# Two loops over groups of tiles and of experts written out in a kernel of four attention and four feed-forward layers

## The reference, cut to what matters

```
x = x + tanh(g_xattn[i]) * xattn_i(layernorm(x), ctx)
x = x + tanh(g_ffn[i])   * ffn_i(layernorm(x))          # i = 0..3
```

```
# ffn_2: 16 experts, 4 chosen per token, hidden width 176, and a shared part
probs = softmax(x @ Wg.T);  w, sel = top_k(probs, 4)
routed = sum over chosen e of w_e * (silu(x @ W1[e].T) * (x @ W3[e].T)) @ W2[e].T

# ffn_3: 64 experts, 8 chosen per token, hidden width 96, at most 128 tokens per expert
g, u = split(x @ gate_up[e]);  out += w_e * (silu(g) * u) @ down[e]
```

## Time and profile before

| | |
|---|---|
| median of 3 runs | 3113.04 us (3112.49 to 3119.17) |
| the profiled execution | 3111.15 us |
| its span, first to last instruction | 3109.1 us |
| busy: PE, DVE, ACT, POOL | 2461.1, 1349.5, 1225.0, 1111.9 us |
| instructions executed in it | 43759 |
| mean granted TensorE clock | 0.897 |

### The profile page before, as it was taken

The page is one execution under the profiler, slowest core; times in us unless marked ns, Lnnn a source line. Parts: engine busy times, 40 slices in busy tenths (PEclk is TensorE's granted clock), DMA queues, the critical chain, the costliest instruction groups (busy, mean ns, idle before and its releaser), DMA issues.

```text
span 3109.1 us, 43759 instructions
## 1 busy us (share of the span) xinstructions
PE 2461.1 (79%) x10553; PEld 1494.0 (48%) x10597; DVE 1349.5 (43%) x3445; ACT 1225.0 (39%) x4408; POOL 1111.9 (36%) x1106
## 2 busy tenths in 40 slices
PE   5999999788888999899999978888758654614553
PEld 4666668443443444466666644444434323303442
DVE  2444333666666333344444324222366645721112
ACT  3444432465465221466555533222245352501211
POOL 3211110333333000243354532344424545446665
PEclk9999999898899999999999989999968876757777
DMA  9900001000001100000000023444431000003655
GB/s 348 350 11 1 1 0 28 10 1 1 1 1 37 64 1 0 1 1 1 1 18 12 30 77 107 88 75 75 75 102 66 1 8 1 8 7 87 146 123 135
DMA packets 159717, 163.21 MB, mean 52 GB/s; under 512 B 27027, under 2 KB 151203, under 8 KB 158772
## 3 DMA queue, kind: packets, MB, share of 16 engines
q1 hardware_dynamic: 127124, 119.64, 12.9%
q0 software_dynamic: 32416, 41.61, 7.2%
HBM read 82.14 MB, written 79.10 MB: 52 GB/s over the span
## 4 chain that ended last, share of the span: by engine, by line
issue 37%; PE 13%; DVE 7%; DMA 4%; ACT 4%; POOL 2%; another core or an unknown queue 1%; SPq 1%; DVEq 0%; POOLq 0%; ACTq 0%
PE ps L133 10%; ACT work L948 2%; DMA moe_sum<-work,weights 2%; DMA work<-xn_rows,weights 1%; PE ps L883 1%; POOL slots L2634 1%; PE ps L2084 1%; DVE n_mx L973 1%; DVE work L2138 1%; DVE xn L249 1%; DVE work L994 0%; ACT weights L2359 0%; POOL moe_sum L2735 0%; ACT work L2113 0%
## 5 line engine op out<-in xcount | busy, mean ns | idle before, releaser
L133 PE MATMUL ps<-work,weights 128*128 128x512 f32 (+5 forms) x2176 | 836.5, 550 | 39.0 <-ACT work L948 14.1
L133 PE MATMUL ps<-xn_T,weights 128*128 (+5 forms) x1392 | 577.2, 555 | 32.2 <-issue 8.4
L133 PEld LDWEIGHTS ps<-work,weights 128*128 128x128 f32 (+3 forms) x2188 | 335.5, 198 | 284.2 <-issue 248.5
L133 PE MATMUL ps<-weights,work 88*128 (+4 forms) x1472 | 404.1, 399 | 47.3 <-DVE work L2782 23.5
L948 ACT ACTIVATE work<-ps,n_negm 128x128 f32<-128x128 f32 (+2 forms) x1024 | 333.3, 354 | 265.9 <-DVE n_rinv L982 170.1
L133 PEld LDWEIGHTS ps<-xn_T,weights 128*128 128x128 f32 (+3 forms) x1392 | 255.9, 196 | 218.0 <-issue 191.4
L1030 POOL TENSOR_TENSOR work<-work,n_rinv 128x512 f32<-128x512 f32 (+2 forms) x256 | 215.1, 852 | 347.6 <-DVE n_rinv L982 347.5
L133 PEld LDWEIGHTS ps<-weights,work 128*128 128x128 f32 (+2 forms) x1472 | 226.9, 195 | 106.1 <-issue 77.9
L714 POOL TENSOR_TENSOR work<-work,rinv 128x512 f32<-128x512 f32 x128 | 133.3, 1042 | 311.0 <-DVE rinv L665 285.0
L948 ACT ACTIVATION_READ_ACCUMULATOR work<-ps,n_negm 128x1 f32 x1024 | 221.4, 220 | 0.0
L883 PE MATMUL ps<-ident,work 128*128 128x128 f32 x768 | 135.0, 304 | 86.4 <-DVE work L968 68.9
(11 more groups left out here) (304 smaller groups left out, 3539.8 us busy)
## 6 DMA issues: line engine op xcount, KB each, us to landing
f_rows<-weights SPq DMA_DIRECT2D x17, 2176.0 KB, 19.5
weights<-in_L_ffn_gate_up_proj SPq DMA_DIRECT2D x16, 768.0 KB
work<-f_rows SPq DMA_DIRECT2D x80, 136.0 KB
weights<-in_L_ffn_W SPq DMA_DIRECT2D x96, 88.0 KB
weights<-in_L_ffn_down_proj SPq DMA_DIRECT2D x16, 384.0 KB
f_sum<-weights SPq DMA_DIRECT2D x2, 2176.0 KB, 15.2
moe_sum<-weights POOLq DMA_DIRECT2D x2, 2176.0 KB
weights<-in_L_xattn_Wo SPq DMA_DIRECT2D x2, 2048.0 KB, 12.4
```

What stands on the lines that cost most here:

```text
L133: return nc.tensor.matmul(out, lhsT, rhs, start=start, stop=stop, skip_group_check=True)
```

## The change

`tiles_first` and `tiles_run` lose their `Fori`; the groups are a Python loop, so that `g` is a number and every wait in them a constant. The tests `isinstance(g, int)` become tests of `g`. The reads of places and expert numbers stay, three repeated ones at each group's start included.

The functions of the last mixture lose their argument `g` and run over all 64 experts. The copies of the tables are gone: gathers, scatters and DVE's scaling read the tables themselves (`f3_idx`, `f3_tab`), so the waits ahead of the copy, `f3_idx_ready` and DVE's wait for it go too. DVE waits once for the table to be read. Each signal is declared once with 64 items where it had 16 items in 4 bodies. The loops over four parts stay as they are.

```
     def tiles_run(engine, F, eng):
         engine(0, True, False)
-        with eng.Fori(1, F.groups, 1) as g:
+        for g in range(1, F.groups):
             engine(g, True, True)
         engine(F.groups, False, True)
...
-        with sp.Fori(1, NG, 1) as g:
+        for g in range(1, NG):
             for q in range(GE // QE):
-                done(sp, f3_y_mm, g - 1, (q + 1) * QE - 1)
+                done(sp, f3_y_mm, 0, (g - 1) * GE + (q + 1) * QE - 1)
                 f3_weights(sp, g, q)
...
-    def f3_pool_start(pool):
+    def f3_gather(pool, e):
+        nc.gpsimd.indirect_dma_start(f3_xe[:, e % XR, :], None, xs, bass.IndirectOffsetOnAxis(ap=f3_idx[:, e, 0:1], axis=0))\
+            .then_inc(f3_gathered[e % XR].sem, 16)
+
+    def f3_pool(pool):
         pool.wait_ge(tab_read, 16)
         pool.wait_ge(xs_stored.sem, 16 * (1 + NS))
-        nc.gpsimd.tensor_copy(f3_idx_g[:, 0:AHEAD], f3_tab_i.bitcast(U32)[:, 0:AHEAD, 0]).then_inc(f3_made, 1)
-        pool.wait_ge(f3_made, 4)
...
-    def f3_pool(pool, g):
-        done(pool, f3_gathered[(AHEAD - 1) % XR], g, 15)
-        done(pool, f3_added[0], g, -1)
-        done(pool, f3_added[1], g, -1)
-        tab = f3_tab_i.bitcast(U32)
-        nc.gpsimd.tensor_copy(f3_idx_g, tab[:, bass.ds(g * GE + AHEAD, GE), 0])
-        nc.gpsimd.tensor_copy(f3_idx_s, tab[:, bass.ds(g * GE, GE), 0])
-        nc.gpsimd.tensor_copy(f3_wt, f3_tab[:, bass.ds(g * GE, GE), 1]).then_inc(f3_idx_ready.sem, 1)
-        done(pool, f3_idx_ready, g, 0)
...
+        for e in range(AHEAD):
+            f3_gather(pool, e)
+        for e in range(L3E):
+            if e + AHEAD < L3E:
+                done(pool, f3_xt_tr, 0, e + AHEAD - XR)
+                f3_gather(pool, e + AHEAD)
+            done(pool, f3_y_ready, 0, e)
+            done(pool, f3_added[e % 2], 0, 16 * (e // 2) - 1)
+            nc.gpsimd.indirect_dma_start(acc[e % 2], bass.IndirectOffsetOnAxis(ap=f3_idx[:, e, 0:1], axis=0), f3_y[:, e % YR, :], None,
...
-    def f3_dve(dve, g):
-        done(dve, f3_idx_ready, g, 0)
-        for j in range(GE + 2):
+    def f3_dve(dve):
+        dve.wait_ge(tab_read, 16)
+        for j in range(L3E + 2):
```

More of the change, by code:

```diff
@@ L2047, in tiles_sp @@
         for j in range(TG):
-            if not isinstance(g, int):
+            if g:
                 done(sp, F.added[j % 2], g - 1, 16 * (j // 2) + 15)
@@ L2105, in tiles_act @@
                 added = 16 * ((e - 4) // 2) + 15
-                if not (isinstance(g, int) and g == 0 and added < 0):
+                if g or added >= 0:
                     done(act, F.added[e % 2], g, added)
@@ L2144, in tiles_pool @@
             done(pool, F.y_ready, g, j)
-            if j >= 2 or not isinstance(g, int):
+            if g or j >= 2:
                 done(pool, F.added[j % 2], g, 16 * (j // 2) - 1)
@@ L2555, in _build @@
     tab_read = semaphore("tab_read")
-    f3_idx_ready = signal("f3_idx_ready", 1, NG)
     f3_w_in = [Signal(semaphore(f"f3_w_in{i}"), 32, NG, 0) for i in range(GE // QE)]
[L2558 to L2566, removed]
+    f3_gathered = [Signal(semaphore(f"f3_gathered{i}"), 16 * L3E // XR, 1, 0) for i in range(XR)]
+    f3_added = [Signal(F2.added[i].sem, 16 * L3E // 2, 1, F2.added[i].end + 16) for i in range(2)]
+    f3_xt_tr = signal("moe_xt_tr", L3E, 1)
+    f3_xt_ready = signal("moe_xt_ready", L3E, 1)
+    f3_gu_mm = signal("moe_g_mm", L3E, 1)
+    f3_sg_ready = signal("moe_sg_ready", L3E, 1)
+    f3_h_ready = signal("moe_h_ready", L3E, 1)
+    f3_y_mm = signal("moe_y_mm", L3E, 1)
+    f3_y_ready = signal("moe_y_ready", L3E, 1)
     x_done = semaphore("x_done")
@@ L2738, in f3_pe @@
[L2738 to L2742, removed]
+        for e in range(AHEAD):
[7 more added lines that the diff above has]
+            nc.gpsimd.indirect_dma_start(acc[e % 2], bass.IndirectOffsetOnAxis(ap=f3_idx[:, e, 0:1], axis=0), f3_y[:, e % YR, :], None,
+                                         bounds_check=(B + 1) * P - 1, compute_op=ALU.add).then_inc(f3_added[e % 2].sem, 16)
@@ L2743, in f3_pe @@
+    def f3_pe(pe):
+        for j in range(L3E + 3):
+            if j < L3E:
+                done(pe, f3_gathered[j % XR], 0, 16 * (j // XR) + 15)
+                done(pe, f3_xt_ready, 0, j - 2)
                 for k in range(KD):
@@ L2941, in _ @@
         f3_route_pool(pool, NS - 1)
-        f3_pool_start(pool)
-        with pool.Fori(0, NG, 1) as g:
-            f3_pool(pool, g)
+        f3_pool(pool)
     @block.tensor
@@ L3009, in _ @@
             f3_route_pe(pe, NS - 1, t)
-        with pe.Fori(0, NG, 1) as g:
-            f3_pe(pe, g)
+        f3_pe(pe)
     @block.scalar
@@ L3072, in _ @@
             f3_route_act(act, NS - 1, t)
-        with act.Fori(0, NG, 1) as g:
-            f3_act(act, g)
+        f3_act(act)
     @block.vector
@@ L3140, in _ @@
             f3_route_dve(dve, NS - 1, t, link)
-        with dve.Fori(0, NG, 1) as g:
-            f3_dve(dve, g)
+        f3_dve(dve)
         f3_end_dve(dve)
```

59 lines of the change are left out of this document (23 added, 36 removed).

## The result

The changed kernel takes 3006.97 us (median of 4 runs, 3003.06 to 3008.07); the kernel before, run beside it, 3114.54 us (4 runs, 3112.49 to 3119.17). The ratio is 0.965, with a 95% interval of 0.9634 to 0.9667. The forecast was 3017, the range 3004 to 3042. The profiled execution took 3008.02 us against 3111.15.

The account below looks back on a forecast made before the run. The prediction took sequencers and the PE-ACT-DVE ring's latency to bound the tile loop, POOL's rate the last mixture. Gains 73.5 + 22.7 = 96.2 us from 3111.15 gave 3015, or 3017 beside the median; range 3004 to 3042.

Parts of the forecast that it names:

- Waits made constant: Tile loop: step falls from 3.45 to 2.55 us a tile, 79 steps 201.4 us; with the edges 73.5 us gained.
- Nine edges of the tile loop: Between groups of the tile loop: 0.6 us an edge remains for repeated reads, 5.4 for nine; bounds nothing and 1.45 each.
- Three edges of the mixture: Between groups of the last mixture: each costs 8.1 us, and all of it goes, 24.2 us.
- Waits at the loads: Last mixture, POOL's waits beside weight loads: 12 x 1.8 = 21.6 us, so 2 us given back; bounds -5 to +5.
- The last six experts: End of the last mixture: priced like every other step, 3.17 us from scatter to scatter, with no gain.
- The start of the mixture: Last mixture's first group: its copies go, but the first scatter waits for the first result; 0.5 us gained, bounds 0 and 1.
- A: Rival, tile loop: scatters bind it, landing 1 us later; step 2.95, 32 us of gain lost, 3049; chance 0.08.
- B: Rival: code fetch stalls, 19 us on PE in the tile loop and 9 us on other engines, 3045; chance 0.07.
- D: Rival: slower than before; some 25 code blocks queue behind transfers, at 5 us each 3142; chance 0.01.
- C: Rival, tile loop: tile loads, not register waits, hold the loop groups; only 30 us gained, 3083; chance 0.03.
- E: Rival: more gain; PE's queue hides the nine edges (5.4) and load waits reach their lower bound (5 + 2), 3005; chance 0.06.

Follow-up runs that it names:

- t3_counted: Changed kernel, but each wait in groups 1 to 9 of the tile loop is its own instruction again and counts `waits_met` up: 3059.74 us, tile loop 262.1.
- t5: Changed kernel, but ACT and DVE run the tile loop as `Fori`; PE, POOL and SP stay written out: 3038.2 us, tile loop 229.7, steps of 2.89.
- t6: Changed kernel, but PE alone runs the tile loop as `Fori`; the other engines stay written out: 3033.68 us, tile loop 263.6, steps of 3.13.
- t4_reads_once: Changed kernel, but PE keeps the expert numbers of a group's last three tiles and doesn't read them again: 2972.64 us, tile loop 201.5.
- m1_edges: Changed kernel, but POOL waits ahead of experts 16, 32 and 48 for all its gathers and scatters, without copies: 2989.2 us, mixture 229.5.
- m5_edges_dve: Changed kernel with POOL's wait at experts 16, 32, 48; DVE also finishes each group and waits for POOL: 2994.48 us, mixture 239.3.
- t2_mixture_only: Kernel before with only the mixture's part of the change; the tile loop keeps its loop: 3088.18 us, ratio 0.9917.
- after_again: Changed kernel itself, run again in the third batch: 2981.94 us, ratio 0.9685 to the kernel before.
- m3_one_expert: Changed kernel, but the last mixture's weights are loaded per expert, each pair of transfers once its place is free: 2952.75 us, ratio 0.9562, mixture 194.7.
- m4_idle_gathers: Changed kernel, but POOL issues six gathers past the last expert that nobody reads: 2985.76 us, mixture 227.0.
- t1_tiles_only: Kernel before with only the tile loop written out; the mixture keeps its loop: 3035.41 us, ratio 0.976.
- b1_both: Changed kernel with expert numbers kept across tile-loop edges and mixture weights loaded per expert: 2947.64 us, ratio 0.9566 to the kernel before.

## Why the prediction was right, step by step

**Waits made constant: right.** 2.55 us a tile, 73.0 us with the edges against 73.5. That the count behind a wait and not the arithmetic makes the cost was argued from the earlier trace rows and is shown by t3_counted, with the standing wait and its count taken as one. That PE's own waits and those of ACT and DVE both have a part is shown by t5 and t6.

**Nine edges of the tile loop: right.** 207.3 - 201.4 = 5.9 us, forecast 5.4, and t4_reads_once shows that it is the reads.

**Three edges of the mixture: right in size** by construction (8.1 was read off), and m1_edges and m5_edges_dve show 5.9 of it; the last 2.2 is not taken apart.

**Waits at the loads: mis-sized.** The prediction took 12 x 1.8 = 21.6 us, 2 more than the 19.8 of before; they came to 27.6, so 7.8 more, past its bound of 5 more. That bound was also worked out wrongly: with "each wait as long as the longest", 12 x 2.7 = 32.4 us, it would have been 12.6 more and have taken in what was measured. Step by step over 3.17, before has in each group three waits of 1.9 us in the mean and a fourth, two experts ahead of the edge, of 0.9. After has twelve at every fourth expert, 2.3 in the mean. The fourth no longer cut short explains some 3 us, and that the prediction had seen. The rest, 0.4 us on each of the twelve, is partly variation: the same mixture has waits of 23.0 us in all in t2_mixture_only, 27.6 after, 27.3 in after_again. With POOL's wait at the edges put back the twelve are 25.1 us (m1_edges) and 27.0 (m5_edges_dve), so the edges, as put back there, hid nothing of it. Which of them a given load meets was not taken further; m3_one_expert shows only that the burst makes them.

**The last six experts: missed.** They have no gather in the changed kernel, which stops at the 64th. In after they take 2982.12 - 2968.44 = 13.68 us, where six steps are 19.0: 5.3 us gained, and m4_idle_gathers takes 5.1 back. The old loop went on gathering 6 experts past the last one, here by its last two operations on POOL:

```profile
3081.68 0.99 POOL L2731 DMA_INDIRECT work<-xn_rows,weights  x1 [0.30 <-issue]
3082.98 1.57 POOL L2735 DMA_INDIRECT moe_sum<-work,weights  x1 [0.30 <-issue]
```

The prediction priced the last experts at 3.17 because they ran so before, and did not ask what the new loop still issues for them. This gain (5.3 us) and the longer waits (5.8 over the 2 that were counted) nearly cancel: the mixture saved 21.8 us, against 22.2 in the sum. That this part of the sum is so near is luck.

**The start of the mixture: undersized,** 2.4 us (19.7 to 17.3 from the last instruction that writes the slots table to the first scatter) against the 0.5 of the prediction. Part is the table load of 1.28 us ahead of ACT's first copy in the loop body before; it is gone after:

```profile
2827.88 1.28 ACT L2768 ACT_TABLE_LOAD   x1 [67.00 <-PE ps L2744]
```

```profile
2750.34 0.38 ACT L2755 ACTIVATE work<-ps 128x256 f32<-128x256 f32 x1 [66.15 <-PE ps L2731]
```

The first is the kernel before, the second the changed one, ACT's first work in the mixture. How the rest of the 2.4 us divides wasn't taken apart.

**What else lies between 3017 and 3007.** The touched stages gave 73.0 + 21.8 + 2.4 = 97.2 us, one more than the sum. Stages that the change doesn't touch were 5.5 us shorter in the profiled run (2.0 ahead of the tile loop, 1.6 in the attention, 1.9 at the end). And the median lay 1.9 above the profiled run before and 1.1 below it after, 3 us more. The sum had nothing for these, some 8.5 of the 10 us by which the forecast was off; their cause is not shown, and between the two runs of t5_pe_out alone lie 21 us. The 1.9 us at the end don't hang on the mixture's code: t1_tiles_only keeps the old mixture and takes 24.2 us there too.

**The rivals.** A: some scatters now do wait for a landing (nine, 12.2 us in all on POOL), but the buffers of results take it up and eight tiles take 21.07 us, so 32 us were not lost. B and D: 13 + 11 = 24 more packets of code are fetched, as many as the 25 blocks of D, and PE stands idle in the tile loop only at the edges' reads (4.0 us) and twice at the last tiles (0.6 and 0.5 us). C fell with t3_counted: the loop is written out there, the tiles are loaded as in the changed kernel, and the slow step is back. E gave 3005, which is nearer to 3007 than the forecast, but not by its mechanism: the edges cost 5.9 us where it had them hidden, and the waits at the loads grew where it had them shrink.

**Left open:** why all kernels of the later batches need some 25 us less between the two mixtures (563 to 567 us against 588 to 595). The traces place it: ahead of DVE's instruction at line 2392, in layer 3's attention, before, after and all kernels of the first batch have two or three waits of 29 to 34 us in all, nearly all put down to "remote", a releaser that the profile can't name, and none of the eight later kernels has them. Before has 34.0 us of them and after 29.9, so at most 4 us between these two profiles can come from there. The record gives the first and the third batch the same chip number and the second another, so the number of the chip doesn't explain it.

## What to carry to other kernels

A wait on a value in a register can cost much more than its arithmetic: in this kernel it stands as its own instruction with a count behind it, and eight of them a tile on PE, with the like on ACT and DVE, took 0.82 of 3.45 us in a ring over the three engines. Where a first group runs with constants, as group 0 here, its trace gives the gain in advance. Where one queue sets the pace with small transfers that wait for each other, try loading the weights in pieces of one expert and not in bursts; here it gave 27 us. When a loop is written out, look also at what it did past its last item.

## What the runs showed of the hardware

- A transfer of 1152 KB in two pieces stretches the time from a scatter to the next on its sum from 6.35 to as much as 9.18 us in the changed kernel; in pieces of a quarter, spread over the experts (m3_one_expert), it leaves it at 6.35.
- 24 more packets of instructions cost PE no stall in the tile loop that the trace shows. The back edge of ACT's loop in layer 3's attention costs 2.4 us as before (from the branch at 2437.1 to the next instruction at 2439.5 in the changed kernel).
- PE's mean granted clock over the mixture was 0.79 in the changed kernel, with PE busy 61% of it, and 0.90 in m3_one_expert, where the waits at the loads are gone and PE is busy 60% of it (117.59 of 195.00 us). b1_both has 0.91, after_again 0.77. What raised it isn't shown:

```profile
2730.00:2925.00 195.00, 117.59 (x722) 99.61 (x720) 42.37 (x124) 39.06 (x120) 155.42 (x120) 0.90 0.75 152
```
